# Two half steps of attention issued together, the first batch prepared at places of its own, and the weight parts spread anew

## The reference

```
h = layernorm(x) * (1 + ca) + sa
x = x + ga * attn0(h)        # 16 heads of 16; q and k RMS-normed and rotated; softmax(q k^T / 4 + 1) v; projection
h = layernorm(x) * (1 + cb) + sb
x = x + gb * ffn0(h)         # ternary weights, silu gate, two 1024x1024 layers with gelu
h = layernorm(x) * (1 + ca) + sa
x = x + ga * attn1(h)        # 16 heads of 16 with biases, norms of the outputs
h = layernorm(x) * (1 + cb) + sb
x = x + gb * experts(h)      # 8 experts of 256 -> 1024 -> 256
```

## Time and profile before

| | |
|---|---|
| median of 3 runs | 2278.61 us (2273.42 to 2293.51) |
| profiled execution | 2290.8 us, its span 2288.8 us |
| mean granted TensorE clock | 0.923 of full |
| PE, DVE, ACT, POOL busy | 86%, 62%, 53%, 26% of the span |
| raw matmuls, maxima | 1024 each, the maxima 689 ns each |
| exponentials | 512, 1022 ns each |

### The profile page before, as it was taken

How to read it: one execution, slowest core, us unless ns; L and a number is a source line. 1 busy time by engine, 2 the same in 40 slices (tenths; PEclk the granted TensorE clock), 3 DMA queues, 4 the chain that set the end, 5 groups by cost and what they waited for, 6 DMA issues and landing times. The chain is left out here.

```text
span 2288.8 us, 33887 instructions
## 1 busy us (share of the span) xinstructions
PE 1961.4 (86%) x12653; PEld 817.4 (36%) x12653; DVE 1418.1 (62%) x2722; ACT 1209.5 (53%) x1686; POOL 604.9 (26%) x520
## 2 busy tenths in 40 slices
PE   4468988999966999999999965999999995688887
PEld 3123333333323444444444431233333332344443
DVE  1478888888824445445435422777888892677672
ACT  1347777778743334234324222567777785556563
POOL 2546666666440000000000011101111100343442
PEclk9769999999987999999999985799999997799999
DMA  3132333443225000000000003333332224222300
GB/s 112 48 63 84 106 89 92 115 114 108 82 90 202 20 1 20 20 1 19 20 3 17 11 33 65 56 66 56 59 59 59 51 37 143 103 102 77 135 35 22
DMA packets 111586, 148.19 MB, mean 65 GB/s; under 512 B 11714, under 2 KB 95027, under 8 KB 109364
## 3 DMA queue, kind: packets, MB, share of 16 engines
q1 hardware_dynamic: 111412, 145.77, 23.4%
HBM read 100.34 MB, written 45.14 MB: 64 GB/s over the span
## 5 line engine op out<-in xcount | busy, mean ns | idle before, releaser
L613 DVE TENSOR_REDUCE A_M<-A_SM 128x1 f16<-128x512 f32 x1024 | 681.8, 689 | 159.8 <-PE A_SM L800 152.4
L462 ACT ACTIVATE A_P<-A_ST 128x1024 f32<-128x1024 f32 x512 | 521.5, 1022 | 153.5 <-PE A_ST L813 149.6
L800 PE MATMUL A_SM<-A_KT,A_QS 48*128 48x512 f16 x1024 | 404.5, 407 | 46.7 <-DVE A_M L613 34.3
L813 PE MATMUL A_ST<-A_QS,A_KT 49*128 49x512 f16 x1024 | 391.9, 395 | 1.8 <-DMA A_QS<-A_MT 1.7
L1165 PE MATMUL B_PA<-B_Hh,B_wh 128*128 128x512 f16 x1024 | 388.1, 379 | 0.0
L1165 PE MATMUL B_PA<-B_Hl,B_wh 128*128 128x512 f16 x1024 | 388.1, 379 | 0.0
L830 PE MATMUL A_AV<-A_P,A_V 128*32 128x256 f32 x4096 | 333.0, 397 | 9.9 <-DVE A_yn L649 7.1
L1069 ACT ACTIVATE B_af<-B_PA,B_sv 128x512 f32<-128x512 f32 x192 | 132.0, 688 | 356.0 <-PE B_PA L1165 355.8
L800 PEld LDWEIGHTS A_SM<-A_KT,A_QS 48*128 48x128 f16 x1024 | 94.2, 93 | 401.9 <-DVE A_M L613 203.6
L1130 DVE TENSOR_SCALAR B_Hh<-B_af 128x512 f16<-128x512 f32 x128 | 57.9, 452 | 269.7 <-ACT B_af L1069 269.7
L1025 POOL TENSOR_TENSOR B_hl<-B_hf,B_hh 128x512 f16<-128x512 f32 x16 | 18.5, 1157 | 548.2 <-ACT B_hh L1052 548.2
(11 more groups left out here) (259 smaller groups left out, 3403.3 us busy)
## 6 DMA issues: line engine op xcount, KB each, us to landing
qk<-A_tr SPq DMA_DIRECT2D x64, 256.0 KB, 2.1
D_w_st<-in_we_dram SPq DMA_DIRECT2D x16, 1024.0 KB, 5.0
A_KT<-qk SPq DMA_DIRECT2D x96, 128.0 KB, 4.3
A_QS<-qk SPq DMA_DIRECT2D x96, 128.0 KB, 4.5
A_w_st<-in_w_ffn_dram SPq DMA_DIRECT2D x32, 352.0 KB, 3.2
w_hi<-A_f_hi SPq DMA_DIRECT2D x32, 176.0 KB, 1.9
w_lo<-A_f_lo SPq DMA_DIRECT2D x32, 176.0 KB, 2.0
B_wl<-w_lo SPq DMA_DIRECT2D x1, 5632.0 KB, 25.3
```

The lines of the kernel that those rows point to most:

```text
L462: nc.scalar.activation(P[:, st, 2 * pair:2 * pair + 2, :], ST[:, u % 2, :, :], ACT.Exp, scale=1.0 / math.sqrt(HD)).then_inc(exp_s, 1)
L613: nc.vector.tensor_reduce(M[G % 2][:, tt, o:o + 1], SM[:, n % 2, :], AX, ALU.max, negate=True).then_inc(max_s, 1)
L800: nc.tensor.matmul(SM[:, n % 2, :], QS[b % 2][r, 2 * g + pair, tt * 128:tt * 128 + 128], KT[b % 2][r, 2 * g + pair, :], start=True, stop=T ...
L813: ins = nc.tensor.matmul(ST[:, u % 2, a, :], KT[b % 2][r, pair, o:o + 128], QS[b % 2][r, pair, :], start=True, stop=True)
```

## The change

- PE in an even step s issues raw(s + 28), both halves of scores(s // 2), and raw(s + 29); then what else belongs to step s. In an odd step it issues only the rest. DVE takes both maxima in the even step. ACT's order isn't touched.
- In layer 0 batch 0 has places of its own: layer norm, projections and rotation 40 steps earlier than before against its scores, its stack jobs H0 to H3 at steps -90 to -84 (before: -78 to -60), the loads from -80 on. The layer norm of batch 1 stands at -198 to -186 (before: -108 to -96). In layer 1 that of batch 1 stands at -92 to -80 (before: -44 to -32).
- Of batch 0 DVE rotates and splits two of the four token tiles (`rotate_first`, `low_first`), in memory borrowed from P; the stack jobs H2 and H3 of batch 0 are copied there too.
- The tokens are loaded ahead of the weights. The split of the weights stands between AGG and RSTD of batch 0 on DVE, the projection's split and the rope tables later. PE waits for w_split only at the first QK, and QK pass p only for h_low of its own half.
- GpSimd fills one KT and one V at the start, the rest after T1 of batch 0.
- The 32 weight parts stand at three per batch for 15 of them (steps 41, 49, 57 of batches 0 to 4), and the other 17 at every seventh step from 358 to 470.

```diff
-AT0 = placed(-160, dict(STAT=(-12, -11, -9, -8), AGG=-7, LNG=-5, RSTD=-4, XN=(-3, -2, -1, 0), T0=2, T1=4, QK0=(14, 16), QK1=(24, 26),
+LAYER_NORM = dict(STAT=(0, 1, 3, 4), AGG=5, LNG=7, RSTD=8, XN=(9, 10, 11, 12))
+AT0 = placed(-172, LAYER_NORM) | placed(-160, PROJECT | ROTATE | STACK0) | dict(YT0=(82,), YT1=(84,), P0=(94, 96), P1=(104, 106))
+AT1 = placed(-108, LAYER_NORM) | placed(-96, PROJECT | STACK1) | dict(YT0=(82,), YT1=(84,))
+EARLY0 = [placed(-212, LAYER_NORM) | placed(-200, PROJECT | ROTATE) | placed(-200, dict(ROT=(35, 41, 52, 53), HI=(44, 50, 56, 58), LOW=(47, 53, 57, 59)))
+          | placed(-90, dict(H0=0, H1=2, H2=4, H3=6, HIGH=tuple(range(10, 18)), LOWS=(18, 19, 20, 21))),
+          placed(-198, LAYER_NORM)]
+EARLY1 = [{}, placed(-92, LAYER_NORM)]
+STAGE_AT = [64 * (i // 3) + (41, 49, 57)[i % 3] if i < 15 else 358 + 7 * (i - 15) for i in range(4 * B)]
...
+            sp.dma_start(xt[:, :, :], d["x_tok"][0, :, :].rearrange("(t p) c -> p t c", p=128)).then_inc(xt_ld, 16)
             sp.dma_start(w_st[:, :, :], d["wqkv"].rearrange("(k p) n -> p k n", p=128)).then_inc(w_ld, 16)
-            sp.dma_start(xt[:, :, :], d["x_tok"][0, :, :].rearrange("(t p) c -> p t c", p=128)).then_inc(xt_ld, 16)
...
+                if s == slots_of("T1", 0)[0] + 4:
+                    initial(1)
+                    initial(2)
+                    if L0:
+                        nc.gpsimd.memset(f_acc[:, :], 0.0).then_inc(f_sum, 1)
+                        pool.wait_ge(f_sum, 1)
...
+            def rotate_first(tt):
...
+                nc.vector.tensor_tensor(u3(ro_v[:, 0, :]), u3(un), tab3(rope[:, tt, 0, :]), ALU.mult).then_inc(q_rot_v, 1)
+                nc.vector.tensor_tensor(u3(ro_v[:, 1, :])[:, :, 0:hd2], u3(un)[:, :, hd2:HD], tab3(rope[:, tt, 1, 0:hd2]),
+                                        ALU.mult).then_inc(q_rot_v, 1)
+                nc.vector.tensor_tensor(u3(ro_v[:, 1, :])[:, :, hd2:HD], u3(un)[:, :, 0:hd2], tab3(rope[:, tt, 1, hd2:HD]),
+                                        ALU.mult).then_inc(q_rot_v, 1)
+                dve.wait_ge(q_rot_v, 4 * k + 3)
+                dve.wait_ge(qk_low, k + 1)
+                nc.vector.tensor_tensor(qo[:, tt % 2, :], ro_v[:, 0, :], ro_v[:, 1, :], ALU.add).then_inc(q_rot_v, 1)
...
-                maximum(s + AHEAD)
+                if s % 2 == 0:
+                    maximum(s + AHEAD)
+                    maximum(s + AHEAD + 1)
...
+                if s == slots_of("AGG", 0)[0] + 1:
+                    split_weights()
...
-            pe.wait_ge(w_split, 2 if L0 else 1)
...
+                if (name, n, p) == ("QK0", 0, 0):
+                    pe.wait_ge(w_split, 1)
...
-                    pe.wait_ge(h_low, FT * (n + 1))
+                    pe.wait_ge(h_low, FT * n + p + 1)
...
-                raw(s + AHEAD)
-                if 0 <= s < SLOTS * B:
-                    scores(s // 2, 1 - s % 2)
+                if s % 2 == 0:
+                    raw(s + AHEAD)
+                    if 0 <= s < SLOTS * B:
+                        scores(s // 2, 1)
+                        scores(s // 2, 0)
+                    raw(s + AHEAD + 1)
```

More of the change, by code:

```diff
@@ L115, in placed @@
     return {name: tuple(base + o for o in (off if isinstance(off, tuple) else (off,))) for name, off in table.items()}
-AT0 = placed(-160, dict(STAT=(-12, -11, -9, -8), AGG=-7, LNG=-5, RSTD=-4, XN=(-3, -2, -1, 0), T0=2, T1=4, QK0=(14, 16), QK1=(24, 26),
[L119 to L126, removed]
+LAYER_NORM = dict(STAT=(0, 1, 3, 4), AGG=5, LNG=7, RSTD=8, XN=(9, 10, 11, 12))
+PROJECT = dict(T0=2, T1=4, QK0=(14, 16), QK1=(24, 26), QK2=(30, 32), QK3=(40, 42), V0=(46, 48), V1=(56, 58))
+ROTATE = dict(SUM=(19, 29, 35, 45), VAR=(30, 46), RMSG=(31, 47), INV=(32, 48), UN=(33, 34, 50, 51), ROT=(35, 41, 51, 57),
+              HI=(44, 50, 60, 66), LOW=(47, 53, 63, 67))
+STACK0 = dict(H0=82, H1=84, H2=98, H3=100, HIGH=tuple(range(98, 106)), LOWS=(108, 109, 110, 111))
+STACK1 = dict(HIGH=(50, 50, 51, 51, 52, 52, 53, 53), LOWS=(54, 54, 55, 55))
+AT0 = placed(-172, LAYER_NORM) | placed(-160, PROJECT | ROTATE | STACK0) | dict(YT0=(82,), YT1=(84,), P0=(94, 96), P1=(104, 106))
[5 more added lines that the diff above has]
+STAGE_AT = [64 * (i // 3) + (41, 49, 57)[i % 3] if i < 15 else 358 + 7 * (i - 15) for i in range(4 * B)]
 AV_AT = ((7, 9), (11, 12), (13, 15), (17, 19))
@@ L147, in at @@
     def at(s, what, i=-1, late=0):
-        n, r = divmod(s - late - AT[what][i], SLOTS)
-        return n if r == 0 and 0 <= n < B else None
+        return when.get((what, i, s - late))
     def group_at(s, late):
@@ L422, in _ @@
                             nc.gpsimd.tensor_tensor(yTl[:, f, :], yT[:, f, :], yTh[:, f, :], ALU.subtract).then_inc(yT_low, 1)
-                    for c in range(4):
-                        k = at(s, "STAGE", c)
-                        if k is not None:
-                            weight_part(4 * k + c)
+                    if s in STAGE_AT:
+                        weight_part(STAGE_AT.index(s))
                 else:
@@ L504, in out_of_bank @@
                     act.wait_ge(job_done, upto(name, n))
-                    if i >= 2:
+                    if i >= 2 and n >= 1:
                         act.wait_ge(hi_st, 32 * n + 32)
@@ L556, in _ @@
                 if L0:
+                    if s == slots_of("QK0", 0)[0]:
+                        act.wait_ge(wp_ld, 16)
+                        nc.scalar.activation(wp_h[:, :, :], wp_st[:, :, :], ACT.Copy, scale=WS).then_inc(w_high, 1)
                     for f in range(FT):
@@ L708, in _ @@
                                                     ).then_inc(q_scaled, 1)
+                    for tt in range(TT):
+                        n = at(s, "ROT", tt)
+                        if n is not None and by_dve(n, tt):
+                            rotate_first(tt)
+                        n = at(s, "LOW", tt)
+                        if n is not None and by_dve(n, tt):
+                            low_first(tt)
             if L0:
```

154 lines of the change are left out of this document (95 added, 59 removed).

## The result

The changed kernel takes 2270.4 us (median of 20 runs, 2265.5 to 2276.8), the kernel before 2282.6 in the runs beside it (median of 20). The ratio is 0.9949 with a 95% interval of 0.9939 to 0.9960: 12 us faster, where 45 were forecast. The profiled execution has a span of 2270.1 us, 18.7 less than before.

The account below looks back on a forecast made before the run. PE was taken to set the pace, with DVE close behind. Terms 15 + 12 - 2 + 3 + 12 + 5 = 45 us off the 2278.6 us median gave 2233.6, forecast 2234, range 2194 to 2266.

Parts of the forecast that it names:

- Pairing +15: Both attentions: two half steps issued together win 37 us on PE, less 22 us of waits; net 15, ends -25 and +40.
- weight parts +13: Attention(0): 12 us from undisturbed refines and clock, less 2 for crowded late parts, plus 3 at the end.
- the 22 us: Both attentions: expected cost of second raws waiting for VectorE's maxima, half of a 44 us bound over 64 groups.
- The term for the late parts: Late batches of attention(0): GpSimd falls behind and YT's low halves queue behind a part; 2 us lost, ends 0 and 10.
- The first batch, +12: Start of layer 0: earlier T0 4 us, QK0 on the first half 1, a later wait 7; ends 3 and 20.
- that is now ready by then: Layer 0 start: batch 1's XN, for which PE waited 13.45 us before 84.61, would be ready in time.
- The 7 us of the later wait: Layer 0 start: 7 of PE's 13.45 us wait won, with two of four tiles on DVE; ends 0 and 13.
- Layer 1, +5: Start of attention(1): STAT and AGG ahead of T0 win 3 us, QK0's first half 2; ends 1 and 7.
- the pairing costs what the rest wins: Rival, both attentions: pairing loses 22 us instead of winning 15; time 2271, within 1%; chance 0.13.
- what was named beforehand as a sign of error: PE's waits for A_M over 30 us per 300, P waiting for yTl in late batches, or DVE's rotation doubling in length.
- the signs that it was right: Raws and scores within 0.3 us, 1.85 us per two job steps, refines under 0.5, T0s near 44 and 73, earlier ends.
- The rival in which the early batch brings nothing: Layer starts: rotations on two engines take turns and loads set the end; time 2248; chance 0.1.

Follow-up runs that it names:

- run 13: The changed kernel with half steps issued one by one and weight parts at their old places: 2279.4 us, ratio 0.9990 to the kernel before.
- run 1: The changed kernel with half steps issued one by one again on PE and VectorE: 2268.9 us, ratio 0.9937 to the kernel before.
- run 9: The changed kernel with weight parts at the old steps 41, 47, 53 and 59 of every batch: 2268.8 us, ratio 0.9942 to the kernel before.
- experiment 5: The changed kernel with ACT's copy ysb one step earlier, ahead of the exponential of step 19: 2253.1 us, ratio 0.9872 to the kernel before.
- experiment 6: The changed kernel with half steps one by one and ACT's copy ysb one step earlier: 2264.8 us, ratio 0.9917 to the kernel before.
- Run 4: The changed kernel with the 17 late weight parts at 8 steps, with gaps where YT's low halves are due: 2259.2 us, ratio 0.9898.
- experiment 3: The changed kernel with GpSimd's memsets of the first batches' stacks waiting for batch 1's XN: 2260.1 us, ratio 0.9905 to the kernel before.
- run 10: The changed kernel with all four tiles of batch 0 rotated by GpSimd alone: 2275.3 us, ratio 0.9966 to the kernel before.
- run 12: The changed kernel with all memsets at the start of GpSimd's queue: 2262.7 us, ratio 0.9930 to the kernel before.
- experiment 11: The changed kernel with a pair's second raw issued at the head of the odd step: 2397.2 us, ratio 1.0506 to the kernel before.

## Why the forecast was too fast by 37 us, step by step

Of the 37 us, 4 are the median of the kernel before (2278.6 in three runs, 2282.6 in twenty). The other 33 are terms of the sum: 12 us were won where 45 were forecast. The change is 2282.6 to 2279.4 for the new places of the first batches, and 2279.4 to 2270.4 for pairs and parts together: 3.2 + 9.0, where 17 + 28 were forecast. The 3.2 isn't told from nothing (run 13's ratio is 0.9990, up to 1.0002).

**Two terms were added that overlap.** Pairing +15 and weight parts +13 stand in the sum as if independent. Each alone comes near its term in the medians, 10.7 and 10.5 us; together they make 9.0 (runs 1, 9, 13). Both shorten the same stretch, batches 2 to 5 of attention(0), where the refine runs beside the last part. That the pairs' 10.7 lies near 15 is luck: the forecast had them win about 1 us in every batch of both layers, and in attention(1) a steady batch is 0.7 us longer. The forecast costed each edit against the kernel before, and never one against the kernel with the other.

**The pairing.** The gain of a pair was right: 1.86 us where 1.85 stood for the two steps with a job. Its make-up was not quite: the job keeps its 0.75 us, and all the gain is in the pair itself, 0.54 for 0.64. The Trainium skill (TensorEngine Tiling (Array Packing), Key Properties) has the engine drained at a change of mode. The job ahead of values keeps its 0.75 us, so the trace agrees. What failed is the step that took PE's 0.12 us per pair as won wherever VectorE could follow; ACT was looked at in the tail only. Six of the sixteen steps of the group shown lie under an unbroken chain of ACT, and a chain that starts with a job is 0.22 us later, not earlier, when the job moves behind the pair. Experiments 1, 5 and 6 show it: the pairs earn 11.7 us once ysb stands ahead of the exponential, and nothing (1.5 us lost, inside the intervals) where it doesn't.

The chain isn't the whole of it. In a steady batch of attention(1) it makes 1.1 us of the difference between paired and unpaired (from +0.7 to -0.4), and 2.2 us are still missing from the 2.6 that were taken as won. The wait that the forecast did name, the second raw behind VectorE's maxima, is the likely rest. In the list of PE's waits it *fell*, from 4.8 to 1.4 per 300 us, but the second raws are late by about 3 us per batch, and pair 8, 0.12 us shorter by the forecast, is 0.21 longer with either place of ysb. How much of the 22 us it cost in all no run separates.

**Weight parts, 12 - 2 + 3.** The refines fell to 0.22 us, 8.9 us in VectorE's sum as forecast, and the end won its 3 us. The batches beside the parts won 13 (2 to 5, run 1 against run 13), near the 12 of the term. The term for the late parts was mis-sized: 2 us (ends 0 to 10) where batches 6 and 7 lose 12.4 (against run 9), 8.7 of it waits for yTl; the rest was not measured by itself, and half clock is seen behind the longest of them. The mechanism was named (GpSimd falls behind, the low halves queue behind a part) and never divided out, although 5.5 us per part against seven steps of 0.8 could have been set side by side. Run 4 gives the 11.3 us back.

**The first batch, +12.** T0 at 44 was right (44.29). The first raw gained 0.6. Batch 1's T0 was forecast near 73, and stands at 82.20. The step that failed is "that is now ready by then". Batch 1's XN was ready, by 58.46; but its norm was taken as free for batch 0, whose evacuation stands behind the norm's Ln on ACT. The edit puts GpSimd's memsets in the same place, and the forecast never asked what else is issued there. That is 5.1 us (experiment 3: T0 at 77.50, first raw at 122.9); with the memsets at the start the first raw is at 121.5, 7.1 of the 12. The 7 us of the later wait were also too many: VectorE ends batch 0's low halves at 82.4, not long before GpSimd's 85.48 of old, since the projections of batch 0 ran at half clock (QK matmuls 0.43 us apart, before mostly 0.22). VectorE's `rotate_first` was not stretched (0.68 and 0.41 us per operation): GpSimd had finished. The split earns 3.3 us (run 10).

After that the path runs over VectorE and batch 2's norm, as shown above. The forecast let that wait keep its place, and no term of the sum asks what it hangs on.

**Layer 1, +5.** It gained 2.1; the same memsets, and experiment 3 makes it 6.4.

Of the rivals, "the pairing costs what the rest wins" gave the nearest time, 2271, but not the cause: each of the two terms took from the other. Of what was named beforehand as a sign of error, one was seen: P waits for yTl in the late batches. PE's listed waits for maxima and the stretch of the rotation stayed away. Of the signs that it was right, the two raws and two scores within 0.3 us held in most pairs, not in every one. The rival in which the early batch brings nothing takes away 14 us where the term is 12; its time would be 2246. One gain was in no step: the 4.9 us of batch 1 of attention(1). They are absent in run 13 too (60.2), and in the unpaired run 1 (60.3), so they belong to the start or to that one profile; this was not settled.

## What to carry to other kernels

When PE's order gains, follow each engine that PE feeds for one full period, and write down which chain has no gap in it: an operation that the new order moves back by 0.2 us is a loss if it heads such a chain, whatever PE wins elsewhere. For an engine that gets work at a fixed spacing, divide: if the work takes as long as the spacing, whatever is queued there with a deadline will miss it. Read lateness from the starts of instructions too: a list of waits leaves out the late one that hides beside another. And cost the edits of one change together: two that mend the same stall don't add, and two that land at the same time, like the norm and the memsets here, can collide though each is harmless alone.

## What the hardware showed

A VectorE `tensor_scalar` on 4 elements per partition took 5.80 us beside four GpSimd memsets in a row, and 5.34, 4.02 and 2.08 in three other places (attention(1), and layers 1 and 0 of run 12), 0.17 alone; each time it ended within 0.05 us of the end of a memset. The Trainium skill (SBUF — State Buffer, Who interferes with whom) says that `tensor_scalar` can enter a mode that takes the shared pair of ports, and that whoever comes second is blocked for the whole instruction; the trace agrees, except that the step here was blocked for four instructions, not one. In layer 0 of run 12 VectorE's split of the weights, with two SBUF inputs, ran beside such a memset at its usual 1.76 us; in layer 1 it is recorded with 3.84, begun while the step before it was still blocked. Four `tensor_scalar` operations of 256 elements took 4.00 us beside GpSimd's rotation, and 1.38 without it.

A matmul on 48 rows cost nothing beside a score on the other rows (0.54 us with it, 0.53 without), and 0.32 us alone (experiment 11). And in the stretch from 44 to 127 us the windows grant the changed kernel a clock of 1.00, while its matmuls of 512 columns stand 0.43 us apart, the pace of 1.2 GHz: there the spacing of the matmuls has to be read, not the column.
